# A graph layer with experts on one core: the value products of the even groups move from the edge pass to the message pass

## What is computed

```python
h = jnp.concatenate([x[dst], x[src], edge_attr], axis=1)
gate = jax.nn.sigmoid(_bn(jax.nn.silu(h @ W1f + b1f) @ W2f + b2f, g_int, beta_int))
msg = gate * (jax.nn.silu(h @ W1m + b1m) @ W2m + b2m)
agg = jax.ops.segment_sum(msg, dst, num_segments=N)
return jax.nn.relu(x + _bn(agg, g_bn, beta_bn))
```

## Time and profile before

| | us |
|---|---|
| median of three runs | 889.56 |
| the profiled execution's own time | 891.85 |
| its span, from the first to the last instruction | 890.0 |
| edge pass on PE, first product to last | 35.8 to 540.5 |
| message pass on PE, first transposes to last sums | 551.6 to 733.7 |
| node norm and experts | from 736 to the end |

### The profile page before, as it was taken

How to read it: one execution, slowest core, us unless ns; L and a number is a source line. 1 busy time by engine, 2 the same in 40 slices (tenths; PEclk the granted TensorE clock), 3 DMA queues, 4 the chain that set the end, 5 groups by cost and what they waited for, 6 DMA issues and landing times. The chain is left out here.

```text
span 890.0 us, 14611 instructions
## 1 busy us (share of the span) xinstructions
PE 801.7 (90%) x4536; PEld 680.6 (76%) x4537; DVE 538.2 (60%) x883; ACT 477.9 (54%) x855; POOL 451.4 (51%) x391
## 2 busy tenths in 40 slices
PE   4579999999999999999999997888779874799998
PEld 3468888888888888888888885666667662799998
DVE  5257655566655555565665543888787874666664
ACT  4135555555555555555555555666557661565661
POOL 2578777666766667666666103556455573100000
PEclk9779999999999999999999996999999995699999
DMA  7778899888888878888889823676575733001201
GB/s 210 238 246 295 290 321 328 317 304 303 295 289 304 297 274 298 297 306 305 302 280 325 328 94 154 227 256 216 184 260 197 265 132 108 1 25 51 91 24 30
DMA packets 67756, 201.74 MB, mean 227 GB/s; under 512 B 10912, under 2 KB 18878, under 8 KB 67726
## 3 DMA queue, kind: packets, MB, share of 16 engines
q0 software_dynamic: 25024, 81.94, 28.3%
q1 hardware_dynamic: 31182, 77.48, 24.8%
q10 hardware_dynamic: 11520, 41.95, 12.3%
HBM read 156.19 MB, written 45.14 MB: 226 GB/s over the span
## 5 line engine op out<-in xcount | busy, mean ns | idle before, releaser
L122 POOL DMA_INDIRECT pre<-table_dst,idx x157 | 159.9, 1019 | 108.2 <-PE p_h L577 56.5
L404 POOL DMA_INDIRECT from_src<-table_src,idx x157 | 162.0, 1032 | 47.9 <-issue 47.9
L568 PE MATMUL p_h<-eaT_hi,w_hi 128*128 128x512 f32 (+1 forms) x320 | 134.4, 420 | 1.7 <-DVE eaT_lo L488 1.7
L568 PE MATMUL p_h<-eaT_lo,w_hi 128*128 128x512 f32 (+1 forms) x320 | 126.2, 394 | 0.0
L568 PE MATMUL p_h<-eaT_hi,w_lo 128*128 128x512 f32 (+1 forms) x320 | 125.8, 393 | 0.0
L494 DVE BATCH_NORM_STATS2 gate_stats<-zg_st 128x512 f32 (+2 forms) x80 | 54.3, 681 | 105.1 <-ACT zg_st L425 104.7
L531 DVE TENSOR_TENSOR h_lo<-h_full,h_hi 128x512 fp32r<-128x512 f32 (+1 forms) x80 | 54.5, 681 | 103.8 <-ACT h_full L451 103.5
L512 DVE TENSOR_TENSOR pre<-pre,from_src 128x512 f32<-128x512 f32 (+1 forms) x157 | 98.6, 688 | 11.9 <-DMA from_src<-table_src,idx 11.9
L577 PE MATMUL p_h<-ident,pre 128*128 128x128 f32 x628 | 95.4, 274 | 11.4 <-DVE pre L512 11.4
L577 PEld LDWEIGHTS p_h<-ident,pre 128*128 128x128 f32 x628 | 78.5, 141 | 33.8 <-DVE pre L512 12.1
L450 ACT ACTIVATE h_hi<-p_h 128x512 fp32r<-128x512 f32 (+1 forms) x80 | 47.1, 588 | 94.9 <-PE p_h L577 94.9
(11 more groups left out here) (213 smaller groups left out, 1876.9 us busy)
## 6 DMA issues: line engine op xcount, KB each, us to landing
z_gate<-zg_st ACTq DMA_DIRECT2D x40, 512.0 KB, 4.4
h_val<-hv_st ACTq DMA_DIRECT2D x40, 512.0 KB, 6.0
hv<-h_val SPq DMA_DIRECT2D x40, 512.0 KB, 5.5
gate<-z_gate SPq DMA_DIRECT2D x40, 512.0 KB, 4.6
ea<-in_edge_attr_dram SPq DMA_DIRECT2D x39, 512.0 KB, 6.9
raw<-in_L_ffn_W_dram SPq DMA_DIRECT2D x16, 512.0 KB, 4.6
pre<-table_dst,idx POOLq DMA_INDIRECT x157, 4.0
from_src<-table_src,idx POOLq DMA_INDIRECT x157, 5.8
```

The lines of the kernel that those rows point to most:

```text
L122: pool.indirect_dma_start(pre[b][0:n, t, :], None, table_dst, bass.IndirectOffsetOnAxis(ap=idx[b][0:n, t:t + 1], axis=0)).then_inc(got_dst ...
L404: pool.indirect_dma_start(from_src[b][0:n, t, :], None, table_src, bass.IndirectOffsetOnAxis(ap=idx[b][0:n, T + t:T + t + 1], axis=0)).the ...
L568: nc.tensor.matmul(p_h1[c][:, 0:w], w1_hl[wp][:, k, c * P:(c + 1) * P], eaT_hl[b % 2][dp][:, k, 0:w], start=n == 0, stop=False)
```

## The change

- The edge pass no longer has `value_layer`, nor what made its operands (ACT 468, DVE 525) or drained it (ACT 461). The hidden layer of every group is stored by ACT right after the gate's product (`store_hidden`, now with both buffers).
- The message pass makes the value product for every group: 12 matmuls of group g + 1 in each step, before the sums of g. `hidden_hi` (ACT) and `split_hidden` (POOL) run for every group, two groups ahead; `message` on DVE (`SCALAR_TENSOR_TENSOR`) runs twice in each step; POOL's multiplication is gone; `msgT` is one buffer, `sigmoid` runs one group ahead instead of two.
- The setup block gathers the destination rows of group 0 only. Those of group 1 follow after the source rows of group 0.

```diff
-                    for b in range(2):
-                        gather_dst(pool, b)
+                    gather_dst(pool, 0)
...
                         if not (first and b == 0):
                             store_gates(g - 1, (b + 1) % 2)
-                            if b % 2 == 0:
-                                store_hidden(g - 1)
+                            store_hidden(g - 1, (b + 1) % 2)
...
-                        if b % 2:
-                            for j in range(KF):
-                                act.wait_ge(v_made, KF * (2 * i + b // 2) + j + 1)
-                                nc.scalar.activation(hv_st[0][:, j, :], p_z[j][:, 0:G], ACT.Identity,
-                                                     bias=vecs[:, 3, j:j + 1]).then_inc(v_copied, 1)
...
-                            if c == KF and b % 2:
-                                value_layer(g - 1, 2 * i + b // 2)
...
-                        if b % 2 and not (last and b == 3):
-                            message(i + (b == 3), (b + 1) % 4)
-                        if b % 2 and not last:
-                            split_hidden(pool, i + 1, b)
+                        if not (last and b >= 2):
+                            split_hidden(pool, 4 * i + b + 2, (b + 2) % 4)
...
-                        if b % 2 and not last:
-                            act.wait_ge(v_psum, KF * (2 * i + b // 2) + KF)
-                            hidden_hi(act, i + 1, b)
+                        if not (last and b >= 2):
+                            act.wait_ge(v_psum, KF * (g + 1))
+                            hidden_hi(act, i + (b >= 2), (b + 2) % 4)
...
-                        if not (last and b >= 2):
-                            sigmoid(i + (b >= 2), (b + 2) % 4)
+                        if not (last and b == 3):
+                            sigmoid(i + (b == 3), (b + 1) % 4)
...
-                            if b % 2 == 0:
-                                message(1, i, b + 1, LAST if last and b == 2 else G)
+                            for j in range(KF):
+                                message(j, g + 1, (b + 1) % 4, LAST if last and b == 2 else G)
...
-                        if b % 2 == 0:
-                            second_layer(1, i, b + 1, LAST if last and b == 2 else G)
-                        elif not (last and b == 3):
-                            second_layer(0, i + (b == 3), (b + 2) % 4, LAST if last else G)
+                        if not (last and b == 3):
+                            second_layer(g + 1, (b + 1) % 2, LAST if last and b == 2 else G)
```

135 lines of the change are left out of this document (45 added, 90 removed).

## The result

The changed kernel takes **846.38 us** (median of four runs, 845.1 to 849.5) against 889.05 us for the kernel before beside it: a ratio of 0.9526, 95% interval 0.9498 to 0.9554. The forecast was 861.0, with a range of 849 to 880. The profiled execution took 849.5 us with a span of 847.5; its terms are compared with those of the 890.0 us span before. Both profiled executions were some 3 us above their medians, so the difference of the spans is still fair.

What follows compares the result with a forecast made beforehand. PE was taken to bound the edge pass, a chain through DVE the message pass. From the 890.0 us span, -56.6, -1.5 and +29.5 gave 861.4, plus 1.85 outside it 863.3; less 2.29, the median was 861.0 us, range 849 to 880.

Steps and rivals of the forecast that it cites:

- value product, 20 x 2.83, and front of the message pass: Edge pass loses 20 products of 2.83 us, -56.6 us; at the message pass's front DVE replaces POOL's multiplication, -1.7.
- start of the edge pass: Fewer gathers ahead of group 0's source rows bring PE's first sums sooner: -1.5 us, bounds -3.4 and +2.
- 38 steps without extras: Ordinary message-pass steps of 5.2 us, with `onehot` held behind POOL's instruction, against 4.62 each before.
- groups with two tiles: Message pass: four groups have a second node tile, adding a second `onehot` and 8 matmuls, 1.6 us each: +6.4 us.
- first step: Message pass: the first step runs at half clock, so its added matmuls and the rest are slow: +2.3 us.
- last step and end: End of the message pass: the two short products stay short, +0.6 us; later stages have no edit, 0.
- Value product out of the edge pass: Edge pass: 20 products of 12 matmuls, 2.83 us each on a PE that never waits, come back as -56.6 us.
- Late next in the edge pass: Edge pass: POOL's gathers and the DMA transfers keep up with groups of 10.97 us, so 0 us is lost.
- two patterns: Message-pass step: `onehot` ahead of POOL gives PE's 4.95 us; POOL ahead holds `onehot` and gives 5.22 us.
- the second pattern: Message pass: POOL goes ahead, `onehot` is held, steps average 5.22 us, and this keeps itself once DVE is delayed.
- the rival: Message pass: `onehot` stays ahead of POOL and PE's own pace sets steps of 4.95 us, total 850 us; chance 0.17.
- What was named and not counted: Message pass: `hvT_hi` waited 16.0 us for `hv` loads, now issued three steps ahead; named as a further gain, not counted.

Runs made afterwards that it cites:

- b_value2: Kernel before with 2 of the 12 matmuls of each value product left in the edge pass, part of the product left out: 843.43 us, ratio 0.9466.
- a_best: Changed kernel with setup again gathering group 1's destination rows and the message pass's first loads issued behind the last edge groups: 841.34 us, 0.9463 of the kernel before.
- after_again: The changed kernel measured again without edits, for comparison on the same chip: 845.57 us, 0.9512 of the kernel before.
- a_late: Changed kernel with the message pass's first hidden-row and gate loads issued behind the last edge groups: 842.50 us, 0.9446 of the kernel before.
- a_dve64: Changed kernel with an added VectorE copy of 64 columns ahead of `onehot` in each message step: 848.47 us, 0.9518 of the kernel before.
- a_dve512: Changed kernel with an added VectorE copy of 512 columns ahead of `onehot` in each message step: 868.14 us, 0.9738 of the kernel before.
- The last experiments: Kernel before with both POOL message-pass instructions shortened (0.9932), ScalarE's hidden-row copy moved behind its message copies (1.0012), or both edits (0.9789), among seven runs.
- a_half: Changed kernel with the later hidden-row and gate loads and POOL's low parts issued as two 512-column instructions: 839.66 us, 0.9418 of the kernel before.

## Why the prediction missed, point by point

By spans, forecast -28.6 us, measured -42.5. Two misses of opposite sign are in this: the message pass came out 23.5 us shorter than forecast, most of it in the ordinary steps (38 x 5.2 against 38 x 4.61), and the edge pass gave 8.8 us less than forecast.

| term | forecast | measured |
|---|---|---|
| value product, 20 x 2.83, and front of the message pass | -58.3 | 2.84 a product (b_value2) |
| start of the edge pass | -1.5 | +1.2 |
| waits and clock inside the edge pass | 0 | +6.0 |
| group 0's transposes, sum of these | -59.8 | -51.0 |
| 38 steps without extras | 38 x 5.2 = 197.6 | 38 x 4.61 = 175.2 |
| groups with two tiles | +6.4 | +7.3 |
| first step | +2.3 | +0.2 |
| 38 steps, against 175.7 | +30.6 | +7.1 |
| last step and end | +0.6 | +1.4 |

- **Value product out of the edge pass: right**, by the trace (10.97 us a group) and by b_value2.
- **Late next in the edge pass, taken as 0: too good by 6 us.** From the first sums to the end of group 38's gate product are 434.6 us against 482.4, 47.8 less where 19 x 2.83 = 53.8 were due. PE's three later waits are 4.5 us of that (the 2.2 near 100 us belong to the start, next point); the slow matmuls behind the last of them are the rest as far as the rows show it. I had looked at long stretches of one rate and at the first groups, not at what SP puts into the queues at the end of the pass. The loads there were in the code, and they cost between 4 us (a_best, which has the other repair as well, beside after_again) and 7 us (a_late's ratio against the changed kernel's, 0.0080).
- **Start of the edge pass: -1.5 forecast, +1.2 in this trace, and small.** The source gathers start at 41.20, not at 34.9: they wait 7.21 us for the stores of the source table, which are issued until 33.59. The landing was estimated at 2.4 us and is 7.6 here, and 4.8 to 5.6 in the eight other traces with this setup, so the -3.3 at the first sums did not come in any of them. By those traces the sums come 1.5 us earlier, and the wait of some 2.2 us near 100 us is the other half of the term, which makes it about +0.7. The +1.2 is an accident of the one execution: its first gather is 1.0 us later than in the trace before, and its source gathers start 2 us later behind the table's stores than in the others.
- **The step of the message pass, taken as 5.2 and measured as 4.61: this is what failed.** The forecast worked out two patterns, 4.95 and 5.22, saw `onehot` due at T+4.7 and POOL's instruction at T+5.05, and then took the second pattern for the sake of one argument: once anything has delayed VectorE, it keeps itself. The trace has `onehot` at T+4.59 and POOL at T+5.09 (565.31 and 565.81 for T = 560.72), close to both numbers. The argument is false for this kernel. A group with two tiles does put POOL ahead, but PE also has 16 sums there instead of 8, so the next transposes come 1.63 us after POOL's start (584.25, 585.88) and the held comparison ends 1.33 us after them. That is before the 12 matmuls are through: PE waits for nothing, POOL's next start waits for these matmuls, and at 590.46 the comparison is first again. It isn't the long group alone that does this: in a_dve64 a held comparison in a group with 8 sums is followed by one that isn't held. a_dve512 shows the other side: where VectorE has 0.68 us more in every step, nearly all comparisons stay held. The forecast said that `onehot`, once held, comes at T+5.3 or later, behind POOL again; measured behind a hold, it comes 0.03 us ahead of the next transposes (590.46, 590.49), since VectorE has by then caught up (its messages waited 0.71 us for the gate).
- **PE's own step was 4.61, not 4.87 to 5.0.** In the sum for PE I took 1.19 us from the sums to the next transposes out of a step in which the sums had waited (rows 5: 596.91 to 598.10). Where they don't wait it is 0.95 us (564.39 to 565.34). A row with a wait in it isn't the price of the engine alone. 38 x 0.34 = 13 us is what this term is off against the 4.95 of the rival, which gave 850; with 4.61 in it the rival would have given 837, and with the 8.8 us that the edge pass lost 846. That the rival's 850 lies so near is thus partly luck: its price for PE was 13 us too high and its edge pass 8.8 us too good.
- **First step:** little of the slow clock was left at 500 us: its transposes take 1.22 us, not 1.94 (1.04 in an ordinary step), and the step is 4.79.
- **Groups with two tiles:** +7.3 instead of +6.4. Some 3.8 of it are the eight more matmuls (0.95 each time, by the step of 5.56), the rest is the hold in three of the four places, and a_half takes 3.4 us away.
- **What was named and not counted:** the 16.0 us of waits for `hv` are gone, as said. The forecast treated them as a share of the 4.62 us before. The last experiments show that they were one of two causes side by side, so they couldn't have been counted by themselves in either kernel.

On the hold, the Trainium skill (SBUF — State Buffer, "SBUF: two separate sides") says that VectorE and GpSimd share a pair of ports as an exclusive lock, taken by whoever starts first. The runs agree: 0.39 us of lead is enough for 0.67 us (561.11; in a_dve64 even 0.11 us), and 0.38 us behind costs 1.89 more (563.01 in a_dve512); a comparison that is held ends 0.53 or 0.54 us behind POOL's instruction, in the kernel before, the changed one and a_dve512.

The fastest version that leaves no work out is a_half: 839.66 us, 0.9418 of the kernel before, interval 0.9387 to 0.9449, below those of the changed kernel and of after_again without overlap. The later loads alone gave 0.9446 with an interval that overlaps with it; that the halved instruction adds something is seen in the 38 steps, 3.4 us shorter, and not in the time.

## What to carry to other kernels

Work out both patterns of two engines that hold each other, and then ask whether the chosen one survives a step in which the engine that is the bound gives the others time to catch up; here that reset the order. Take an engine's own pace only from stretches in which it waited for nothing. When one cause is taken away and nothing happens, look at what now starts in its place before calling it innocent; here only two edits together moved the time by more than 0.7%.
